# Seven attention steps per sequence: one exponential 1024 wide in place of two of 512

## What is computed

```
scores = jnp.einsum('bhqd,bhkd->bhqk', q, k) / np.sqrt(HEAD_DIM)
bias = rel_bias[bucket_ids]                       # by distance of query and key
attn = jax.nn.softmax(scores + bias[None], axis=-1)
out = jnp.einsum('bhqk,bhkd->bhqd', attn, v)
```

## Time and profile before

| | |
|---|---|
| median of 3 runs | 2854.99 us |
| lowest and highest | 2853.36 and 2856.19 us |
| profiled execution, its own time | 2854.48 us |
| its span in the trace | 2852.6 us |
| granted clock of PE, mean | 0.982 of full |
| PE busy | 2752.4 us (96%) |
| ACT busy | 1775.8 us (62%) |
| DVE busy | 2115.9 us (74%) |
| POOL busy | 1266.7 us (44%) |
| exponentials (L1430) | 2048, busy 1109.6 us |

### The profile page before, as it was taken

The page is one execution under the profiler, slowest core; times in us unless marked ns, Lnnn a source line. Parts: engine busy times, 40 slices in busy tenths (PEclk is TensorE's granted clock), DMA queues, the critical chain, the costliest instruction groups (busy, mean ns, idle before and its releaser), DMA issues.

```text
span 2852.6 us, 53205 instructions
## 1 busy us (share of the span) xinstructions
PE 2752.4 (96%) x19426; PEld 1526.9 (54%) x19426; DVE 2115.9 (74%) x4444; ACT 1775.8 (62%) x3799; POOL 1266.7 (44%) x1764
## 2 busy tenths in 40 slices
PE   7989999999999999999999999999999999999998
PEld 5733376433864348643486434854358533585334
DVE  6679756897568965689666995669956799567993
ACT  5438854488545875458754687536875378653785
POOL 3415544355433554335543445434454345433553
PEclk9979999999999999999999999999999999999999
DMA  7160001600025000250002400033000330003300
GB/s 191 31 133 2 24 9 41 137 17 24 9 50 128 17 31 1 60 119 17 31 1 74 105 17 31 1 90 88 17 31 10 101 69 17 31 30 89 60 2 16
DMA packets 71428, 139.16 MB, mean 49 GB/s; under 512 B 12784, under 2 KB 49696, under 8 KB 70016
## 3 DMA queue, kind: packets, MB, share of 16 engines
q1 hardware_dynamic: 69152, 135.29, 19.1%
q10 hardware_dynamic: 2016, 0.45, 0.1%
HBM read 86.02 MB, written 38.82 MB: 44 GB/s over the span
## 4 chain that ended last, share of the span: by engine, by line
PE 71%; DVE 14%; issue 6%; POOL 5%; SPq 1%; ACT 1%; DMA 1%; POOLq 0%; DVEq 0%; ACTq 0%
PE psum L868 20%; PE psum L924 16%; DVE mx L1755 6%; PE psum L643 5%; PE psum L991 3%; PE psum L899 3%; PE psum L831 3%; PE psum L647 2%; PE psum L707 2%; PE psum L683 2%; PE psum L1085 2%; PE psum L1082 2%; DVE nrm L1590 2%; PE psum L1058 1%; POOL X L1872 1%
## 5 line engine op out<-in xcount | busy, mean ns | idle before, releaser
L1755 DVE TENSOR_REDUCE mx<-psum 128x1 f32<-128x512 f32 x2048 | 1266.2, 685 | 87.4 <-PE psum L868 87.0
L1430 ACT ACTIVATE Z<-psum 128x512 f32<-128x512 f32 x2048 | 1109.6, 598 | 279.7 <-PE psum L899 252.6
L1964 POOL TENSOR_TENSOR Z<-Z,W_low 128x256 f32<-128x256 f32 (+1 forms) x1152 | 713.0, 642 | 687.2 <-ACT Z L1430 679.9
L868 PE MATMUL psum<-SK,SQ 63*128 63x512 f32 x2048 | 801.2, 471 | 28.5 <-DVE mx L1755 23.0
L899 PE MATMUL psum<-SQ,SK 64*128 64x512 f32 x2048 | 758.6, 472 | 8.1 <-DMA SQ<-mrow 7.5
L924 PE MATMUL psum<-Z,Vx 128*17 128x256 f32 x8192 | 642.0, 388 | 0.4 <-POOL Z L1964 0.4
L868 PEld LDWEIGHTS psum<-SK,SQ 63*128 63x128 f32 x2048 | 330.0, 191 | 480.8 <-DVE mx L1755 357.9
L899 PEld LDWEIGHTS psum<-SQ,SK 64*128 64x128 f32 x2048 | 311.4, 189 | 79.9 <-ACT Z L1430 37.5
L924 PEld LDWEIGHTS psum<-Z,Vx 128*17 128x17 f32 x8192 | 138.3, 95 | 334.8 <-issue 274.8
L1909 POOL TENSOR_TENSOR Z<-Z 128x512 f32<-128x512 f32 x64 | 83.6, 1306 | 295.6 <-DVE Z L1645 295.6
L1872 POOL TENSOR_TENSOR X<-X,mixed 128x512 f32<-128x512 f32 x64 | 80.4, 1268 | 235.3 <-DVE mixed L1611 235.3
(11 more groups left out here) (138 smaller groups left out, 3716.8 us busy)
## 6 DMA issues: line engine op xcount, KB each, us to landing
W_low<-bias_rows SPq DMA_DIRECT2D x8, 2048.0 KB, 8.6
parts<-Z SPq DMA_DIRECT2D x32, 512.0 KB
W_low<-low_parts SPq DMA_DIRECT2D x7, 1536.0 KB, 6.7
X<-L_attn_a_x SPq DMA_DIRECT2D x8, 1024.0 KB, 5.6
SQ<-parts SPq DMA_DIRECT2D x32, 256.0 KB, 7.9
SK<-parts SPq DMA_DIRECT2D x32, 256.0 KB, 10.7
SQ<-parts SPq DMA_DIRECT2D x16, 512.0 KB, 6.6
SK<-parts SPq DMA_DIRECT2D x16, 512.0 KB, 14.5
```

Of the source, the lines that this page charges most:

```text
L868: pe.matmul(row_bank(c), SQ[rows_of(h, MAX_ROW), h // 2, i * P:i * P + P], SK[rows_of(h, MAX_ROW), h // 2, 512 * k:512 * k + 512], start=T ...
L1430: nc.scalar.activation(ring[:, n % RING, :], col_bank(n), ACT.Exp)\
L1755: nc.vector.tensor_reduce(mx2[:, blk % 2, col, k:k + 1], row_bank(2 * u + k), AX_X, ALU.max)\
L1964: nc.gpsimd.tensor_tensor(ring[:, n % RING, a:z], ring[:, n % RING, a:z], band_exp[:, 4 * hg + cols_of(s)[i], at:at + z - a], ALU.mult)\
```

## The change

In steps 53 to 59 the two columns of a half step go into adjacent banks, and one exponential reads both banks and writes two slots of the ring. It waits for both columns and then counts two events on `e_p`. The rotation over the four banks starts at another one: column 4s + 0 to 3 were in banks 3, 4, 5, 2 and are in 4, 5, 2, 3. All other steps keep their exponentials of 512.

```
-        COL_BANKS = [(3, 4, 5, 2)[n % 4] if n // 4 in WIDE else 3 + n % 3 for n in range(4 * NS)]
+        COL_BANKS = [(4, 5, 2, 3)[n % 4] if n // 4 in WIDE else 3 + n % 3 for n in range(4 * NS)]
...
-                        need(act, e_s, b, n + 1)
-                        nc.scalar.activation(ring[:, n % RING, :], col_bank(n), ACT.Exp)\
-                            .then_inc(e_p.sem, 1)
+                        if s in WIDE and i % 2 == 0:
+                            first = COL_BANKS[n]
+                            need(act, e_s, b, n + 2)
+                            nc.scalar.activation(ring[:, n % RING:n % RING + 2, :], psum[:, first:first + 2, :], ACT.Exp)\
+                                .then_inc(e_p.sem, 2)
+                        elif s not in WIDE:
+                            need(act, e_s, b, n + 1)
+                            nc.scalar.activation(ring[:, n % RING, :], col_bank(n), ACT.Exp)\
+                                .then_inc(e_p.sem, 1)
```

## The result

The changed kernel takes 2860.08 us (median of 20 runs, 2857.8 to 2866.5; four of them lie at 2864.8 and above), the kernel before 2854.86 us (median of 20 runs): ratio 1.0021, 95% interval 1.0014 to 1.0028. It is slower by 5.2 us, which lies at the edge of what I called "the same". I had forecast 2859.5. The profiled execution of the changed kernel took 2860.21 us, 5.7 above that of the kernel before.

The account below looks back on a forecast made before the run. PE was taken as the bound, with ACT close behind. 2854.5 us plus 5.0 (step 60) minus 0.5 (step 53) gave 2859.0, or 2859.5 as median; the 8-in-10 range was 2854.6 to 2863 us.

Parts of the forecast that it names:

- the same: Total time within 0.2%, 5.7 us, of the kernel before; given 72%, with slower at 24% and faster at 4%.
- The bound: Middle of steps 53 to 59: PE sets the pace at 0.98 to 0.99 us per half step, ACT slightly faster.
- Rival A: Seven steps 53 to 59: ACT sets the pace, so half steps shrink; total 2850 to 2854 us; chance 4%.
- The price of a wide exponential: On ACT: 1.035 us start to end, holding ACT 0.91 to 0.92 us, saving some 0.05 us a pair.
- +4.9 us: Total of the sum redone with the skill's formula, given as 8 x (0.64 - 0.03).
- Steps 54 to 59: nothing: Middle steps: PE keeps its beat, with 0.28 us to spare on banks and POOL covered by 0.4 at least.
- Step 53: a gain of 0.06 us: Copy of the maxima 0.06 us earlier, so step 56 starts 0.06 earlier; -0.5 us over eight sequences.
- Step 60: a new wait of 0.63 us: First column, bank 3, waits for the last wide exponential of step 59; +5.0 us over eight sequences.
- Whom I blamed: At step 60: the new bank rotation together with a wide exponential releasing both banks late; wait 0.63 to 0.64 us.
- Sum: Whole kernel: 2854.5 + 5.0 - 0.5 = 2859.0 us profiled, 2859.5 us as median, +0.16%.
- B: After step 60: the new wait costs nothing in the end, through unseen slack or earlier release; 2854.5 to 2855 us; 10%.
- C: Wide steps: the wide exponential holds ACT beyond PE's 0.985 us and sets the pace; 2867 us; chance 7%.

Follow-up runs that it names:

- wide, rotated on: The changed kernel, but from step 60 on the three banks start one further (4, 5, 3, 4): 2855.24 us, ratio 1.0000 to the kernel before.
- Banks alone: The kernel before with only the new bank rotation (4, 5, 2, 3) in steps 53 to 59, all exponentials 512 wide: 2859.98 us, ratio 1.0023.

## Why the prediction was right, point by point

**The bound.** Right. PE's beat of 0.98 to 0.99 us in steps 54 to 59 did not move when ACT's work in them shrank, neither in the changed kernel nor in "wide, rotated on". Rival A, with ACT as the pace, falls with this, although ACT had looked as full as PE in the earlier trace rows.

**The price of a wide exponential.** From start to end I took 1.035 us, measured 1.025. For how long it holds ACT I took 0.91 to 0.92. With the copy L1401 behind it that is right (0.92); with another wide exponential behind it, it is 0.96 to 0.97. So a pair saves next to nothing on ACT: the four exponentials of 512 in step 59 take 2.07 us (starts 0.49, 0.48 and 0.48 apart, the last 0.62 long), the two wide ones 1.99, and the first wide one starts 0.06 us later after its columns. From the formula of the Trainium skill, "ScalarE: Activation LUTs", section "What ACT_TABLE_LOAD costs", I had estimated 1039 ns and 0.95 us between two; the trace has 1025 and 0.96 to 0.97, so for the distance of two wide ones the estimate was nearer than my value from the rows. For two of 512 the same formula would give 0.52 us, and the traces have 0.48 to 0.49. What I worked out with it, +4.9 us, was also added up wrongly: with 1.039 and 0.95 us the steps of my own sum give a wait of 0.67 us at step 60 and no gain at step 53, +5.3 us.

**Steps 54 to 59: nothing.** Right, and shown by two experiments within 0.1%. Less lay between it and a loss than I had said: POOL's band of step 58 starts 0.40 us later and not 0.15, and where no wait of PE covers it, in "wide, rotated on", it is done 0.23 us before `weigh` needs it, not 0.4.

**Step 53: a gain of 0.06 us.** Wrong in sign, small in size: step 56 begins 0.055 us later. I had the copy of the maxima 0.06 us earlier and it came 0.05 later. Two terms of the chain were too small. I had the first wide exponential start 0.60 us after its columns; it started 0.65 after them (mean of eight sequences), because it starts 0.15 us after the second column ends, where one of 512 starts 0.10 after the first; why is not shown. And I let the second one start when its columns were there, because I took ACT to be free at 1735.50; with 0.96 to 0.97 us of hold it was not. Seen from the kernel before, 0.04 of the 0.055 us come with the rotation alone, since four exponentials of 512 behind a later first pair bring the copy nearly as late.

**Step 60: a new wait of 0.63 us.** Right in place and mechanism, 0.72 in size. The missing 0.09 comes from the same two terms: I had the second exponential of step 59 start 0.53 us after its columns, and it started 0.63 us after them, some 0.06 of it because the first one started later and 0.04 because it held ACT for longer. The shorter duration (1.025 and not 1.035 us) gives back 0.01. Of eight such waits my sum had 5.0 us and the traces have 5.7.

**Whom I blamed.** Here the prediction was only half right. The text ahead of it names the exponential that counts as "the second wide one of that step", and the prediction's bounds for the wait, 0.62 to 0.75, hung on the length of a wide exponential alone. It gave no time for the rotation with exponentials of 512. Banks alone shows a wait of 0.73 to 0.74 us, if anything a little longer than with the wide ones: the last of four exponentials of 512 ends about as late as the second wide one. I could have read that in the earlier trace rows: the last two exponentials of step 59 start at 1748.33 and are over 1.10 us later, at 1749.43; with the 0.05 of PE's reaction that is 0.75 us after PE was ready at 1748.73.

**Sum.** +5.0 - 0.5 = +4.5 us forecast, +5.7 + 0.4 = +6.1 in the traces, +5.2 in the medians (+5.8 when repeated). The two errors of my sum have one sign, and the medians came out between. That 2859.5 was hit to 0.6 us is therefore in part luck. The medians and the traces do not contradict each other: in every experiment the traces' sum lies inside the interval of the runs (here 4.0 to 8.0 us). They differ by up to 1.7 us, and in one and the same kernel the stretch from the first to the last row score of a sequence lasts 181.6 to 183.4 us (kernel before, seven sequences), so differences of this size drown in it.

**The rivals.** B (given back later) falls: the wait of step 60 is still whole at the last column of step 63, and the next sequence starts late too: from the last row score to the first one of the next sequence it takes 167.24 us before and 168.09 in the changed kernel (means of seven). In the two kernels without waits in steps 61 to 63 the gain reaches the total. C (a new pace) falls: 0.97 us is below PE's 0.985, but by 0.02 us only; two per cent more and it would have been the pace.

## What to carry to other kernels

Where the rotation of buffers changes its length, look at the border: the first user of a buffer in the new rotation should meet the oldest of the old one, and a table of "last use" for the few columns around the border shows it at once. A larger instruction on an engine that was not the bound brought nothing here, and the buffers that had to be renumbered for it cost more than it could have brought. When a change has two parts, price each of them alone at the suspected place, even if one looks like mere preparation of the other.

## What the runs showed of the hardware that I had not expected

Two adjacent exponentials of 1024 out of PSUM follow each other 0.955 to 0.976 us apart where their columns are there, two of 512 0.476 to 0.495 apart: per element they are the same within about 2%. In step 59 two of 512 hold ACT for 0.97 us (1747.36 to 1748.33) and a wide one for 0.96 (1751.60 to 1752.56). What a wide one saves in its own duration, 1.025 us against two times 0.598, is thus nearly all hidden already when exponentials of 512 stand in line, and the 50 ns a pair that I had expected were in truth about 10.
